# Large transfers begun by ScalarE, odd V tiles in K's PSUM bank, and a search shifted by one slot

## What is computed

```python
x = L0_attn_x                      # (2, 4096, 512)
xn = _layernorm(x, axis=-1)
x = x + attn(xn) + moe(xn)
# attn: windows of 64 rows, 16 heads of 32
qkv = xw @ qkv_w + qkv_b
attn = softmax(q @ k.T * scale + rel_pos_bias)
out = (attn @ v) @ proj_w + proj_b
# moe: 8 experts; each takes its 1024 best rows
scores = (x_flat @ Wg.T).T
top_vals, token_idx = jax.lax.top_k(scores, 1024)
token_w = softmax(top_vals)
h = silu(xg @ W1.T) * (xg @ W3.T)
y = (h @ W2.T) * token_w
out.at[token_idx].add(y)
```

## Time and profile before

| | us |
|---|---|
| median of 3 runs | 2067.52 |
| lowest and highest | 2063.33, 2068.68 |
| the profiled execution | 2065.82 |
| its span, first to last instruction | 2064.0 |

### The profile page before, as it was taken

One profiled execution on the slowest core, in us unless ns is written; L12 is line 12 of the kernel. 1 busy time (PEld: TensorE's weight loads), 2 busy tenths in 40 slices (PEclk: granted clock), 3 DMA queues, 4 the chain that ended last, 5 costly groups with the idle time before them and its releaser, 6 DMA issues.

```text
span 2064.0 us, 39502 instructions
## 1 busy us (share of the span) xinstructions
PE 1958.5 (95%) x16627; PEld 1579.3 (77%) x16627; DVE 1179.3 (57%) x1688; ACT 588.8 (29%) x891; POOL 598.0 (29%) x410
## 2 busy tenths in 40 slices
PE   7999999999888989998899999999999999999997
PEld 5677776767766777776688888888888888888886
DVE  7667677877768788776744544346344543444221
ACT  3222222222223333322433242232332333323221
POOL 1455444444344444444022021211212112112111
PEclk9999999999999999999999999999999999999999
DMA  7444467566643223333444253233532434325311
GB/s 193 130 142 138 134 185 194 160 162 185 177 116 100 68 61 93 104 89 107 163 100 109 78 133 92 58 108 88 129 81 61 126 81 101 93 70 142 61 21 21
DMA packets 182517, 229.91 MB, mean 111 GB/s; under 512 B 35680, under 2 KB 107744, under 8 KB 182368
## 3 DMA queue, kind: packets, MB, share of 16 engines
q1 hardware_dynamic: 168032, 194.26, 32.6%
q0 software_dynamic: 14336, 33.56, 9.1%
HBM read 127.08 MB, written 51.38 MB: 86 GB/s over the span
## 4 chain that ended last, share of the span: by engine, by line
PE 52%; DVE 0%; POOL 0%; ACT 0%; issue 0%; POOLq 0%
PE ps_e L59 17%; PE ps_e L61 17%; PE ps_e L60 17%; PE ps_e L157 1%; POOL out_rows L1683 0%; DVE xn L1836 0%; DVE xgt_lo L1841 0%; ACT x_res L1751 0%; DVE w_lo L1830 0%; DVE got L165 0%; POOLq L1682 0%
## 5 line engine op out<-in xcount | busy, mean ns | idle before, releaser
L59 PE MATMUL ps_e<-xgt_hi,w_hi 128*128 128x512 f32 x1024 | 404.7, 395 | 8.1 <-DVE xgt_lo L1841 8.1
L61 PE MATMUL ps_e<-xgt_hi,w_lo 128*128 128x512 f32 x1024 | 399.5, 390 | 0.0
L60 PE MATMUL ps_e<-xgt_lo,w_hi 128*128 128x512 f32 x1024 | 399.4, 390 | 0.0
L1862 DVE TENSOR_TENSOR hm<-ps_e,silu 128x512 f32<-128x512 f32 x128 | 88.5, 691 | 457.3 <-PE ps_e L61 456.6
L59 PE MATMUL ps<-xt_hi,wqk_hi 128*128 128x512 f32 x512 | 215.2, 420 | 38.3 <-DVE v_sb L1249 37.3
L59 PEld LDWEIGHTS ps_e<-xgt_hi,w_hi 128*128 128x128 f32 x1024 | 192.9, 188 | 46.9 <-DVE xgt_lo L1841 8.8
L1683 POOL DMA_INDIRECT out_rows<-x_res,idx x64 | 100.6, 1572 | 430.0 <-ACT x_res L1751 415.5
L61 PEld LDWEIGHTS ps_e<-xgt_hi,w_lo 128*128 128x128 f32 x1024 | 192.7, 188 | 40.6
L60 PEld LDWEIGHTS ps_e<-xgt_lo,w_hi 128*128 128x128 f32 x1024 | 193.1, 189 | 38.3
L186 POOL DMA_INDIRECT x_in<-xn_rows,idx x64 | 76.4, 1194 | 484.4 <-DVE idx L178 309.5
L60 PE MATMUL ps<-xt_lo,wqk_hi 128*128 128x512 f32 x512 | 208.5, 407 | 0.0
(11 more groups left out here) (187 smaller groups left out, 3354.3 us busy)
## 6 DMA issues: line engine op xcount, KB each, us to landing
pt<-pn_sb SPq DMA_DIRECT2D x496, 64.0 KB
x_f<-in_w SPq DMA_DIRECT2D x48, 512.0 KB
raw<-in_w SPq DMA_DIRECT2D x48, 512.0 KB
x_res<-in_x SPq DMA_DIRECT2D x16, 1024.0 KB, 5.5
out_rows<-x_res SPq DMA_DIRECT2D x16, 1024.0 KB
xn<-x_in SPq DMA_DIRECT2D x256, 64.0 KB, 2.0
xn_rows<-xt_plain SPq DMA_DIRECT2D x9, 1024.0 KB, 4.2
x_in<-xn_rows SPq DMA_DIRECT2D x28, 256.0 KB, 4.8
```

The source lines that it names most:

```text
L59: nc.tensor.matmul(out, w_hi, x_hi, start=start, stop=False)
L60: nc.tensor.matmul(out, w_hi, x_lo, start=False, stop=False)
L61: return nc.tensor.matmul(out, w_lo, x_hi, start=False, stop=stop)
L1862: v.tensor_tensor(hm[:, m % 2, :], ps[:, 2 * (m % 2) + 1, :], silu[:, m % 2, :], ALU.mult).then_inc(hm_ready, 1)
```

## The change

Four things are changed together.

First, the six kinds of 1 MB transfer `load_x`, `keep_xn`, `store_out`, `load_res`, `load_x_ahead` and `keep_xn_ahead` are begun by ScalarE, in its own queue and at places in its own order, with the same waits. SyncE keeps the probabilities' transfers, the reading back (`load_back`, `load_back_ahead`), the scores and the weights. In the later chunks `load_back` moves from the chunk's start to behind the second set of probabilities.

Second, V tiles 1 and 3 go to bank 7 (KB). TensorE waits for K's eviction before them, and the wait for V's eviction moves from before Q to before K.

Third, the search's first step moves from n = 2 to n = 3 of chunk 10 and all later steps by one place; the fifth count matmul moves behind output tile 3 and its `take` to the chunk's end, and choosing and placing shift with them. VectorE empties V tile 1 before it adds the terms or prepares a step, and V tile 3 before it prepares one.

Fourth, GpSimd adds the residual bias in one piece, after the second `normalise` of a chunk.

```diff
@@ tables
-        V_BANK, P_BANK, FINAL_BANK = (0, QB, 0, QB), (0, 1, QB, KB), (0, 1, 2, 3)
+        V_BANK, P_BANK, FINAL_BANK = (0, KB, 0, KB), (0, 1, QB, KB), (0, 1, 2, 3)
-            return 5 * (c - HUNT) + n - 2
+            return 5 * (c - HUNT) + n - 3
@@ SyncE, each chunk
-                if n < FAR:
-                    load_x(n)
+                spread_probs(s - 2)
                 if c == HUNT:
                     load_terms()
-                if FAR <= n < NCH:
-                    load_back(n)
-                spread_probs(s - 2)
-                load_res(c - 1)
                 if FAR < j <= NCH:
                     load_back_ahead(j - 1)
                 spread_probs(s - 1)
-                if n < FAR:
-                    keep_xn(n)
+                if n < NCH:
                     load_back(n)
                 spread_probs(s)
-                if FAR <= j < NCH:
-                    load_x_ahead(j)
...
-                store_out(c - 1)
-                if FAR <= j < NCH:
-                    keep_xn_ahead(j)
@@ ScalarE, chunk
                 o_hi_part(s - 3, 1)
+                if FAR < j <= NCH:
+                    keep_xn_ahead(j - 1)
+                if n < FAR:
+                    load_x(n)
+                load_res(c - 1)
...
                 k_part(s + 1, 1)
+                if n < FAR:
+                    keep_xn(n)
                 o_hi_part(s - 1, 3)
+                if j == FAR:
+                    act.wait_ge(xn0_stored, 2 * 16 * TT * NQ)
+                if FAR <= j < NCH:
+                    load_x_ahead(j)
...
                 o_hi_part(s, 0, projected=TT * c)
+                store_out(c - 1)
                 exponentials(s + 2)
@@ GpSimd, chunk
                 normalise(s - 1)
-                residual(c - 1, (0, 1))
...
                 normalise(s)
-                residual(c - 1, (2, 3))
+                residual(c - 1)
@@ TensorE
                 if t % 2:
-                    pe.wait_ge(q_ready, G * c + t // 2 + 1)
+                    pe.wait_ge(k_ready, G * c + t // 2 + 1)
...
-                pe.wait_ge(v_ready, TT * c + 2)
                 project_q(s + 1, 1)
                 hunt(c, 2)
+                pe.wait_ge(v_ready, TT * c + 2)
                 project_k(s + 1, 1)
...
+                project_q(s + 2, 2)
                 pe.wait_ge(v_ready, TT * c + 4)
-                project_q(s + 2, 2)
...
-                hunt(c, 5)
                 lists_of(5)
                 project_out(c - 1, 2)
...
                 project_out(c - 1, 3)
+                hunt(c, 5)
@@ VectorE, hunt_chunk
                 turn_probs(s - 1)
+                v_part(c, 1)
+                prepare(c, 2)
+
+                add_bias(s, 0)
+                o_lo_part(s - 2, 2)
                 if c == HUNT:
                     add_terms()
-                prepare(c, 2)
-                v_part(c, 1)
-
-                add_bias(s, 0)
-                o_lo_part(s - 2, 2)
                 take(c, 2)
...
                 turn_probs(s)
+                v_part(c, 3)
                 prepare(c, 4)
...
-                add_bias(s + 1, 1)
                 o_lo_part(s - 1, 3)
+                add_bias(s + 1, 1)
                 turn_blocks(c + 1, *range(KC))
                 take(c, 4)
...
                 finish_rows(c - 1, 3)
                 o_lo_part(s, 0)
+                take(c, 5)
+                if choosing:
+                    take_base(SLOT)
+                    place()
                 normaliser(s + 2)
```

More of the change, by code:

```diff
@@ L492, in _ @@
             spread(nc, sp, lists)
-            store_out(NCH - 1)
+            sp.wait_ge(out_ready, TT * NCH)
+            sp.dma_start(d["out"][NCH - 1], x_res[:, :, :]).then_inc(out_stored, 16)
         @block.gpsimd
@@ L614, in split_hi, with load_x, keep_xn, store_out @@
                 nc.scalar.activation(units[u][1], RAW[u % 3], ACT.Copy).then_inc(raw_hi, 1)
+            def load_x(c):
+                if c >= 2:
+                    act.wait_ge(k_mm, G * (c - 1))
+                act.dma_start(rows[c % 2][:, :, :], d["x"][c]).then_inc(x_loaded, 16)
+            def keep_xn(c):
+                act.wait_ge(xn_ready, TT * (c + 1))
+                act.dma_start(d["xn"][c], xt_plain[c % 2][:, :, :]).then_inc(xn_stored, 16)
+            def store_out(c):
+                act.wait_ge(out_ready, TT * (c + 1))
+                act.dma_start(d["out"][c], x_res[:, :, :]).then_inc(out_stored, 16)
+            def load_res(c):
+                if c == 0:
+                    act.wait_ge(raw_lo, ALL_SPLIT)
+                else:
+                    act.wait_ge(out_stored, 16 * c)
+                act.dma_start(x_res[:, :, :], d["x"][c]).then_inc(res_loaded, 16)
+            def load_x_ahead(j):
+                if j > FAR:
+                    act.wait_ge(turned_f, KC * (j - FAR))
+                act.dma_start(x_f[:, :, :], d["x"][j]).then_inc(xf_loaded, 16)
+            def keep_xn_ahead(j):
+                act.wait_ge(xnf_ready, TT * (j - FAR + 1))
+                act.dma_start(d["xn"][j], xt_f[:, :, :]).then_inc(xnf_stored, 16)
             def first_xt_hi(c):
@@ L779, in _ @@
             o_hi_part(s + 1, 1)
+            load_res(NCH - 1)
             probs_t_part(s + 2)
@@ L1090, in chunk @@
                 pv(s + 1, 1)
+                slot_read(c, 5)
                 scores(s + 3)
@@ L1407, in hunt_chunk @@
                     dve.nop(nofuse=True).then_inc(top_ready, 1)
+                if choosing:
+                    choose()
                 turn_probs(s)
+                v_part(c, 3)
                 prepare(c, 4)
+                if listing:
+                    then(v.tensor_scalar(part_i, pos_i, 7, None, ALU.logical_shift_right))
+                    then(to_experts(lists.slot_a, part_i))
+                o_lo_part(s - 1, 3)
+                add_bias(s + 1, 1)
+                turn_blocks(c + 1, *range(KC))
+                take(c, 4)
                 if choosing:
```

59 lines of the change are left out of this document (12 added, 47 removed).

## The result

The changed kernel takes 2083.9 us (median of 4 runs, 2072.16 to 2092.84), the kernel before 2065.43 (median of 4, 2062.62 to 2068.68). The ratio is 1.0092, 95% interval 1.0069 to 1.0114: slower by some 19 us, where 2037 was forecast. The profiled execution of after is its fastest, 2072.16 us with a span of 2070.4, so its trace holds 6.4 us of the loss (2070.4 - 2064.0), and the other runs lost more.

The account below looks back on a forecast made before the run. TensorE was taken to bound the kernel, with recoverable gaps and half-clock matmuls only in attention, before 987 us. Search 18 (net of chunk 14), chunks 5 to 9 9, chunks 1 to 4 -1, chunk 15 2.5: 28.5 off 2065.8, 2037 us; range 2012 to 2058.

Parts of the forecast that it names:

- large transfers on ScalarE's queue: Chunks 5 to 9: probabilities no longer queue behind megabytes and land 4.5 us sooner per chunk; 9 us gained, ends 0 and 22.
- the rival on this point: Chunks 5 to 9: probabilities land no sooner as the DMA engines are busier, no gain there; 2044 us, chance 0.20.
- Term +9: Chunks 5 to 9: 9 us gained from the earlier landing of the probabilities, after deductions for VectorE and the reading back.
- term -1 for chunks 1 to 4: Chunks 1 to 4: 1 us gained from V waits, 2 lost in chunk 4 to load_x_ahead beside the reading back.
- the slower rival: K's eviction, late on ScalarE, stops odd V tiles 1.5 us twice a chunk in 13 chunks; about 2076 us, chance 0.10.
- The search: Chunks 10 to 13: fewer waits and earlier finished rows gain 20 us; 2 lost in chunk 14, net 18, ends 10 and 30.
- The V bank: Odd V tiles in K's bank: nearly all waits for V's eviction go; new wait for K near 0, at most 1.5 us a chunk.
- Reading back beside load_x_ahead: Chunks 5 to 8: load_x_ahead shares the DMA engines with the reading back and lengthens it 2 us, ends 0 and 4.6.
- ScalarE's issues: Beginning transfers costs ScalarE 0.4 to 0.6 us each, where it is idle; its new waits taken at 0.
- Chunk 15: Its 14 slow matmuls stand behind a V wait; 2.5 of 7.3 us gained.
- The residual in one piece: GpSimd's addition after the second normalise is hidden by its wait for the third maximum; 0.
- the second rival: Probabilities still take 12 us to land in chunks 5 to 9, which gain nothing; 2044 us, chance 0.20.

Follow-up runs that it names:

- res_late: The changed kernel with load_res begun by ScalarE after K's first eviction, not at the chunk's start: 2078.94 us, ratio 1.0073.
- pieces_first: all_on_sp with, in chunks 5 to 9, keep_xn_ahead behind the probabilities' pieces of s-2 and load_back_ahead behind those of s-1: 2033.01 us, ratio 0.9841.
- queue_only: The kernel before with only the queue part, the six kinds of 1 MB transfer begun by ScalarE: 2087.41 us, ratio 1.0123.
- bank_only: The kernel before with only V tiles 1 and 3 in K's bank and the waits that go with it: 2065.66 us, ratio 1.0009.
- pieces_first_all: pieces_first with the search chunks' reading back and chunk 10's terms also behind the probabilities' pieces: 2029.91 us, ratio 0.9834.
- q_bank: The changed kernel with V tiles 1 and 3 back in Q's bank and their waits back before Q: 2076.0 us, ratio 1.0063.
- search_only: The kernel before with only the shifted search and VectorE's new order in chunks 10 to 13: 2048.47 us, ratio 0.9924.
- act_after_pv: act_timed with keep_xn_ahead and load_res begun by ScalarE later, behind the split of the attention's output: 2067.2 us, ratio 1.0019.
- all_on_sp: The changed kernel with all transfers begun by SyncE again, in the order of the kernel before: 2050.13 us, ratio 0.9937.
- act_timed: The changed kernel with keep_xn_ahead and load_res after K's first eviction, load_x_ahead after the reading back, load_back_ahead behind the pieces of s-1: 2051.84 us, ratio 0.9929.

## Why the prediction failed, point by point

**The failed step: large transfers on ScalarE's queue.** The sum had the landing fall from 12.05 to about 7.5 us in chunks 5 to 9 and stay at 7.55 in chunks 1 to 4. It stayed at 11.8 to 12.1 in the first and rose to 10.4 to 11.6 in the second. I read the two levels of the earlier trace rows as standing in a queue. They go with the bytes in flight: two megabytes ahead of the pieces in chunks 5 to 9 (keep_xn_ahead and load_x), only load_x in chunks 1 to 4. Those two cost the same from ScalarE's queue (res_late, 11.6 to 13.0 us) as from the pieces' own (before, 10.7 to 12.7), and the landing is 7.1 to 7.6 where keep_xn_ahead goes behind the pieces (pieces_first). The rows held the hint: the rival on this point says "for the same bytes", but by the earlier trace rows it is some 10.7 MB a chunk in chunks 5 to 9 against 7.8 (an estimate, GB/s by length). What I counted at nothing was load_res: in the earlier trace rows it stands behind the eighth piece, and SyncE's program order kept it there. On another engine nothing holds it back, and it started with load_x ahead of the pieces. Term +9 measured -7.9; term -1 for chunks 1 to 4 measured -19.6. queue_only prices the part alone at -25 us.

The Trainium skill, "DMA: Bandwidth & Descriptors", section "Issuing engines are not separate DMA queues", was the rule weighed against the forecast: transfers of several engines interleave on the same DMA engines, and a second issuer saves only issue time. The 10.3 against 10.1 us bear it out for this pair; with three megabytes the spread over the queues did move the landing (11.9, 13.8 and 16.4 us). My rival by it had the right cause but stopped at "no gain" (2044 us); the loss comes from the order given up. The same page of the Trainium skill, section "Queues, rings and completion order", has each DMA engine take turns between the queues that it has work for. The trace agrees in part: in chunk 7 of after both queues moved bytes in the same 6 us, and the pieces landed 3.4 us ahead of load_res. But for 6.0 us before that none of their packets moved. I had taken from the turns that the pieces would pass at once, and this gave the forecast; the passing saved next to no time against the earlier trace rows (11.9 against 12.05 us, with one megabyte more in flight).

**The chance of the slower rival.** It said K's eviction would stop the odd V tiles, 1.5 us twice a chunk, 2076 us. The waits came, 1.9 us at most, 14.4 in 8 waits, once a chunk and not twice, and the odd V tile's 0.06 us of cover was as thin as I said. But its trigger was not ScalarE's DMA waits: it was VectorE's chain behind the late landing (chunk 2 above; in bank_only they stand only where the landing is late, and pieces_first_all has none over 0.4 us). And the bank is the smaller part: putting it back (q_bank) gave 6 to 8 us, with overlapping intervals. So 2076 was near the measured time for a reason that held only in part, which is luck. I gave "slower" 0.10 because I had a mechanism for late evictions and none for late pieces; a rival in which the landing of chunks 1 to 4 takes the value of chunks 5 to 9 could have been read from the same rows.

**The search: right in its sum.** Forecast 20 gained in chunks 10 to 13 (7, 6, 5, 2) and 2 lost in chunk 14; measured 18.0 (7.6, 3.4, 2.9, 4.1) and 1.7. Chunks 11 and 12 gave about half of what was forecast and chunk 13 twice, so that the sum agrees so well is partly luck; chunk 11 takes 60.8 us, not 58. The steps hold in kind: DVE's waits for counts went, and scores(s+2) then waits for the finished rows, 14.3 us in 4, the limit I named. The attribution was off: I gave part of it to the V bank, and search_only gets the same sum without; the bank's share is in chunk 13, over 3 us.

**The V bank.** "Nearly all waits of this kind go": right (33.1 us in chunks 5 to 13 alone, 1.8 in all now). "Near 0" for the new wait: wrong while the pieces are late. Alone the bank is worth 0 (bank_only), once the pieces are on time 4.6 us by the medians, with overlapping intervals. The parts don't add: alone 25 lost, 17 gained and 0 make 8 us lost, and 18.5 was measured. Of the 10 left, q_bank accounts for 6 to 8; the rest isn't placed.

**Reading back beside load_x_ahead.** Taken at 2 us, ends 0 and 4.6. Measured 3.3 in chunk 4 (10.2 against 6.9), 2.9 against the 7.9 of the earlier trace rows in chunk 6, and nothing in chunks 5 and 7 (7.4 and 8.2). In res_late it is 2.5 to 4.5 in all four. Within the bounds, low by half where it happens.

**ScalarE's issues.** 0.4 to 0.5 us each as taken, some of load_res 0.8 and 1.2, hidden: act_after_pv has the same chunks 1 to 4 as pieces_first. The second queue by itself costs nothing that shows there.

**Chunk 15**: 1.0 gained, 2.5 taken. **The residual in one piece** was not run alone. all_on_sp has it and the bank on top of search_only and takes 2050.13 us against 2048.47, so nothing shows of either, as taken for the residual.

**The signs named beforehand.** Waits for v_sb under 5 us: 1.8, as said. normalise(s-1) in chunk 7 at 8 us, or 12 for the second rival: 11.9. Gate waits of 2 to 4 us in chunks 5 to 8: 1.1, 5.8, 0.4 and 0. Waits for k_sb over 10 us as the sign of the slower rival: 14.4. So two signs spoke for rivals, and the size of the loss in chunks 1 to 4 was in none of them.

## What to carry over

When a transfer is moved to another engine's queue, write down what it stood behind in the old one: that order may be what keeps large transfers off the small ones that the critical chain waits for. In ScalarE's program nothing held load_res back until the pieces had gone. Compare the landing time of the small ones with the number of megabytes in flight at their issue before believing in queueing. Here putting the pieces of s-2 and s-1 ahead of every megabyte but load_x, in one queue, gave 20 us over the same kernel without it (2050 to 2030), while the second queue as the change used it lost 32 to 34.

## What the runs showed of the hardware

- With one 1 MB load begun 2 us ahead of eight 64 KB transfers, these had landed some 7.6 us behind their first issue. A second 1 MB load ahead moved this to 10.1 us from the same queue, and to 10.3 us from a second engine's queue. With three megabytes ahead it was 11.9, 13.8 or 16.4 us, by how they were spread over the two queues.
- Eight 64 KB transfers in a queue of their own, behind three megabytes of another engine's queue, moved no packet for 6.0 us, and then landed 3.4 us ahead of the last of the three (chunk 7 of after).
- Reading 1 MB back took 7 to 8 us alone in its stretch. With another 1 MB load begun within 1 us of it, it took 10.2, 10.8, 11.4 and 11.6 us (chunks 4 and 6 of after and of res_late); with the load 2.3 us behind it 7.4 and 8.2 in one kernel, 10.3 and 11.8 in the other.
- A megabyte begun 4.4 to 5.4 us behind the first of the eight pieces, at the issue of the last, still delayed their landing in six chunks of nine (10.0 to 11.7 us) and not in three (7.1 to 7.6). What decides, the trace doesn't show.
- Runs of one kernel spread differently: 2072 to 2093 us in 4 runs of after and 2038 to 2058 in 9 of act_timed, against 2032 to 2034 in 4 of pieces_first. That it goes with ScalarE's queue isn't shown: before, all on SyncE, spreads from 2057 to 2072 in 19 runs.
